# GpSimd makes the one-hots of the deep ranks for the tile that follows (graph aggregation with sampled neighbours, one core)

## What is computed

```
vals, idx = top_k(where(A != 0, -arange(N), -inf), 25)
agg = max over the valid neighbours of X[idx]
agg = where(degree <= 25, maximum(agg, 0), agg)
out = relu(concat([X, agg]) @ W + b)
return layernorm(X + out)
```

## Time and profile before

| | |
|---|---|
| median of three runs | 594.37 us |
| profiled execution | 593.69 us |
| its span, first to last instruction | 592.0 us |
| PE, VectorE (DVE), ACT, GpSimd (POOL) busy | 501.7, 529.4, 396.1, 288.7 us |
| instructions | 13844 |
| length of a batch in the middle | some 67 us |

### The profile page before, as it was taken

One profiled execution on the slowest core, in us unless ns is written; L12 is line 12 of the kernel. 1 busy time (PEld: TensorE's weight loads), 2 busy tenths in 40 slices (PEclk: granted clock), 3 DMA queues, 4 the chain that ended last, 5 costly groups with the idle time before them and its releaser, 6 DMA issues.

```text
span 592.0 us, 13844 instructions
## 1 busy us (share of the span) xinstructions
PE 501.7 (85%) x4544; PEld 340.4 (58%) x4544; DVE 529.4 (89%) x973; ACT 396.1 (67%) x751; POOL 288.7 (49%) x462
## 2 busy tenths in 40 slices
PE   1347899989988999889988999889987999889982
PEld 0115576556654677556755667556754667556761
DVE  5647999999998989999999999999998999998894
ACT  3362567657985688657886589657885589546654
POOL 2552365257633575247733566337742376336700
PEclk9998999899998999899999999899998999899997
DMA  8893244456536644366556555475445462021102
GB/s 257 212 219 105 79 133 118 99 128 160 132 75 171 135 129 101 106 156 165 113 115 173 124 113 136 96 162 171 110 117 141 135 135 65 2 60 38 50 9 73
DMA packets 91810, 71.31 MB, mean 120 GB/s; under 512 B 63651, under 2 KB 80294, under 8 KB 91686
## 3 DMA queue, kind: packets, MB, share of 16 engines
q1 hardware_dynamic: 85286, 56.77, 39.6%
q0 software_dynamic: 6400, 13.12, 8.1%
HBM read 50.99 MB, written 4.19 MB: 93 GB/s over the span
## 4 chain that ended last, share of the span: by engine, by line
PE 37%; DVE 36%; issue 12%; DVEq 7%; DMA 4%; ACT 2%; SPq 1%; POOL 0%; POOLq 0%
PE pair L1038 29%; DVE part L781 16%; DVE hot L776 5%; DVE g_feat L854 4%; DMA adj_sb<-in_adj 4%; DVEq L851 3%; DVE g_val L822 2%; DVE agg_t L881 2%; PE misc L1083 2%; DVEq L920 1%; PE p_V L1022 1%; DVE g_score L824 1%; PE misc L1084 1%; DVE hot_high L776 1%; DVEq L988 1%
## 5 line engine op out<-in xcount | busy, mean ns | idle before, releaser
L1038 PE MATMUL pair<-hot,x_part 128*128 128x128 bf16 (+3 forms) x3120 | 411.0, 280 | 37.3 <-DVE part L781 27.9
L1038 PEld LDWEIGHTS pair<-hot,x_part 128*128 128x128 bf16 x3120 | 239.1, 99 | 145.1 <-issue 51.6
L781 DVE TENSOR_REDUCE part<-pair 128x128 f32<-128x1024 f32 (+1 forms) x256 | 279.4, 1100 | 30.0 <-PE pair L1038 28.5
L479 POOL DMA_INDIRECT g_feat<-in_x,g_idx x200 | 193.6, 968 | 131.9 <-issue 86.5
L526 POOL TENSOR_TENSOR y_sb<-relu_sb,x_sb 128x128 f32<-128x128 f32 x64 | 30.0, 469 | 146.2 <-ACT relu_sb L652 145.7
L598 ACT ACTIVATE V<-p_V 128x512 bf16<-128x512 f32 x98 | 57.7, 589 | 64.9 <-PE p_V L1022 64.7
L626 ACT ACTIVATE hot<-V,first_bias 128x1024 bf16<-128x1024 bf16 x56 | 63.9, 1141 | 25.3 <-PE pair L1038 25.3
L776 DVE TENSOR_SCALAR hot<-V 128x1024 bf16<-128x1024 bf16 x224 | 80.3, 380 | 0.0
L591 ACT ACTIVATE mask<-adj_sb 128x1024 bf16<-128x1024 uint32 x56 | 58.7, 1048 | 21.9 <-DMA adj_sb<-in_adj 21.9
L641 ACT ACTIVATE hot<-distance,one 128x1024 bf16<-128x1024 bf16 x56 | 63.9, 1141 | 0.2
L634 ACT ACTIVATE distance<-V,second_bias 128x1024 bf16<-128x1024 bf16 x56 | 63.6, 1135 | 0.0
(11 more groups left out here) (88 smaller groups left out, 408.8 us busy)
## 6 DMA issues: line engine op xcount, KB each, us to landing
adj_sb<-in_adj SPq DMA_DIRECT2D x56, 512.0 KB
g_adj<-in_adj SPq DMA_DIRECT2D x8, 512.0 KB, 4.4
x_sb<-in_x SPq DMA_DIRECT2D x8, 512.0 KB, 4.6
out<-y_sb SPq DMA_DIRECT2D x7, 512.0 KB, 5.2
g_feat<-in_x,g_idx POOLq DMA_INDIRECT x200
maskT<-mask SPq DMA_TRANSPOSE x56
out<-y_sb SPq DMA_DIRECT2D x1, 448.0 KB, 3.0
w_sb<-in_W SPq DMA_DIRECT2D x1, 128.0 KB, 6.2
```

The lines of the kernel that those rows point to most:

```text
L479: pool.indirect_dma_start(out=g_feat[w][:, k, :], out_offset=None, in_=x_rows, in_offset=bass.IndirectOffsetOnAxis(ap=g_idx[w][:, k:k + 1] ...
L781: dve.tensor_reduce(part[:, par(q, s), :, p], slots_of(q, s, p).rearrange("f k i -> f i k"), AX.X, ALU.max).then_inc(s_used, 1)
L1038: last = pe.matmul(dst, x_part[:, q, part_no, kb], one_hot, start=(first and part_no == 0), stop=(final and part_no == PARTS - 1))
```

## The change

Ranks that exist in the first one or two blocks only (no block from the third on has them; `NARROW` = 2) are made by GpSimd in place of VectorE, by the same tensor_scalar. `WIDE[s]` is the number of the other ranks: 6 in tile 1, 5 in tiles 2 and 3, 4 in 4 to 7. Those from rank 2 to `WIDE` - 1 stay on VectorE: 4, 3 and 2 a tile. `NARROWS` is 6, 4 and 3. GpSimd makes them first in its step s, for tile s+1, and signals `s_narrow`, for which PE waits beside `s_hot`. The 25 gathers are split 6, 6, 6, 3, 4 over steps 1 to 5.

```diff
+NARROW = 2
-    HOTS = {s: DEPTHS[s][0] - ACT_RANKS for s in DEPTHS}
+    WIDE = {s: sum(any(d > r for d in DEPTHS[s][NARROW:]) for r in range(DEPTHS[s][0])) for s in DEPTHS}
+    HOTS = {s: WIDE[s] - ACT_RANKS for s in DEPTHS}
+    NARROWS = {s: DEPTHS[s][0] - WIDE[s] for s in DEPTHS}
...
-            GATHER = -(-K // 5)
+            GATHERS = (0, 6, 12, 18, 21, K)
...
-                gather(0, s_g0, range(GATHER * (s - 1), min(GATHER * s, K)))
+                gather(0, s_g0, range(GATHERS[s - 1], GATHERS[s]))
...
+            def narrow_hots(i, q, s):
+
+                m = pos(i, q, s)
+                wait(s_V, 2 * m + 2)
+                if m >= 2:
+                    wait(s_pair, picked_two_before(i, q, s))
+                for r in range(WIDE[s], DEPTHS[s][0]):
+                    blocks = sum(d > r for d in DEPTHS[s])
+                    dst = hot[:, par(q, s), r, 0:blocks] if r < LOW else hot_high[:, par(q, s), r - LOW, 0:blocks]
+                    pool.tensor_scalar(dst, V[:, q, s - 1, 0:blocks], float(r + 1 - MARK), None, ALU.is_equal
+                                       ).then_inc(s_narrow, 1)
...
                 for s in range(1, NT):
-                    if s <= 5:
+                    nxt = ahead(i, q, s, 1)
+                    if nxt:
+                        narrow_hots(*nxt)
+                    if s < len(GATHERS):
                         gather0(i, q, s)
...
             split_bias()
+            narrow_hots(0, 0, 1)
             run(step)
...
-            one_hots(0, 0, 1, range(ACT_RANKS, DEPTHS[1][0]))
+            one_hots(0, 0, 1, range(ACT_RANKS, WIDE[1]))
...
-                if ranks_needed(s, p) > max([ACT_RANKS] + [ranks_needed(s, g) for g in range(p)]):
-                    pe.wait_ge(s_hot, hot_no(i, q, s, ranks_needed(s, p)))
+                needed, seen = ranks_needed(s, p), max([ACT_RANKS] + [ranks_needed(s, g) for g in range(p)])
+                if needed > seen and seen < WIDE[s]:
+                    pe.wait_ge(s_hot, hot_no(i, q, s, min(needed, WIDE[s])))
+                if needed > seen and needed > WIDE[s]:
+                    pe.wait_ge(s_narrow, narrow_no(i, q, s, needed))
```

More of the change, by code:

```diff
@@ L243, in build @@
         s_hot = sem("onehots_ready")
+        s_narrow = sem("narrow_onehots_ready")
         s_pair = sem("picked")
@@ L302, in hot_no, with narrow_no @@
             return 2 * each * i + each * q + sum(HOTS[t] for t in range(1, s)) + r - ACT_RANKS
+        def narrow_no(i, q, s, r):
+            each = sum(NARROWS.values())
+            return 2 * each * i + each * q + sum(NARROWS[t] for t in range(1, s)) + r - WIDE[s]
         def ranks_needed(s, p):
```

## The result

The changed kernel takes **639.79 us** (median of six runs, 637.9 to 641.7) where the kernel before took 594.32 beside it: a ratio of 1.0775 (95% interval 1.0744 to 1.0806). The forecast was 598, with a range of 582 to 607. Slower was right, by 5 us; it is slower by 45. The profiled execution spans 637.5 us (592.0 before) at a mean granted clock of 0.936 (0.973 before).

What follows compares the result with a forecast made beforehand. VectorE was taken to bound tiles 6 and 7 through tile 1 of the next batch, PE elsewhere. A new wait of 2.0 us less 1.39 saved gives +0.6 a batch, +5 in eight: 598 us, range 582 to 607.

Steps and rivals of the forecast that it cites:

- What VectorE gives up on the path: Narrow one-hots made in VectorE's bound stretch, tiles 5, 6, 7 and 1: 1.72 us a batch, 13.8 in eight.
- It turns on one price: GpSimd's cost c of a 128-column one-hot decides: zero change at c = 0.41, full gain at c = 0.28.
- +0.6 us a batch: Change of the batch period: VectorE's new wait of 2.0 us in tile 6 less 1.39 saved behind it.
- The price of GpSimd's one-hots: Steps 2 to 5, ahead of the last gather: 0.45 us for 128 columns, 0.70 for 256, 6.85 a batch.
- The landing: After the last gather ends, its rows take up to 2.0 us to land before VectorE's maximum in tile 6.
- VectorE's savings: VectorE behind its new wait in tile 6: 0.33 + 0.63 + 0.43 = 1.39 us saved a batch.
- The blocking rival: VectorE and GpSimd block one another: 0.11 us more on each of 13 instructions, 609 us; chance 0.09.
- The signs of being wrong: Gather-to-maximum room above 2.2 us in most batches, VectorE's wide one-hots past 0.6 us, or PE waiting for GpSimd's one-hots.
- ACT gets nothing new: ACT's work is unchanged; it takes the later first split only a tile later; costed at nothing.
- Rank 3's later gap: Tiles 4 to 7: rank 3's wide one-hot comes one gap later, some 1.3 us late in tile 6, covered by PE's idle 5.6.
- Late narrow one-hots for PE: GpSimd's steps 2 to 5 pile up and PE waits in tile 5, some 1 us a batch more: 606; chance 0.04.
- Gathers in time: No new VectorE wait in tile 6: 580.6 us whole, 587.5 halfway; chance 0.22 in time or nearly.

Runs made afterwards that it cites:

- the table that takes lateness away: Changed kernel with the 25 gathers split 9, 5, 5, 3, 3 over steps 1 to 5 in place of 6, 6, 6, 3, 4: 605.2 us against 594.2 before (1.019).
- the paced run: Changed kernel with each piece of GpSimd's two splits waiting for the piece before it: 647.8 us beside a kernel before at 593.0 (1.094).

## Why the prediction was wrong

**Right.** What VectorE gives up on the path, 13.8 us in eight batches, agrees with the runs with 19 gathers (12, and 15 with rank 3 in its old gap); no run gave anything near the 43 us of the forms. The place was right too: the one-hots queue ahead of the gathers, and VectorE waits for the last one in tile 6. "It turns on one price" was right in kind.

**The step that failed** is the sum "+0.6 us a batch": the wait of 2.0 less 1.39. It should have been +6.3 in the mean. In the fifth batch, 8.1 in place of 0.6, its terms were:

- *The price of GpSimd's one-hots*, 6.85 us ahead of the last gather. From start to start they take 2.5, 2.0, 2.4 and 2.2 us in steps 2 to 5 (280.18 less 277.65, and so on), 9.2 in all: +2.3. An undisturbed one takes some 0.50 (128 columns) and 0.84 (256: 277.65 to 278.49), near my upper 0.53 and 0.80; 9 x 0.50 + 4 x 0.84 = 7.86, and the other 1.3 came where single ones took up to 1.24 beside VectorE. With these undisturbed prices my own sum gives +1.6 us a batch, 606, so that the price alone is far from the 45 us. What was absorbed came out as forecast (9.2 - 6.5 = 2.7 for my 1.24 + 1.53). I had put 0.45, between an fp32 TENSOR_SCALAR that stood alone and a run of another operation; the row of the same operation and width, 526 ns, was the one to take.
- *The landing*: 3.60 from the last gather's start to the maximum, not 0.94 + 2.0: +0.7.
- *VectorE's savings*, 1.39 a batch. The rest of the loop is 16.70 us for 16.66 before, in the mean 0.3 shorter: +1.4 here, 1.1 in the mean. Of the 1.39, 0.33 + 0.63 were to shorten this rest. VectorE does have fewer instructions there, but it now waits 1.24 us for PE's picks at 337.17 (1.19 to 1.25 in four of the six batches, none before). PE is late by then: it had started late behind the held maximum, waited 2.15 us for rank 3's one-hot and run at the lower clock; what each of these costs no run separates. Where the gathers are in time (tiles 6, 7, 1, 2 only) the rest is 15.99. The other 0.43, of tile 1, falls where the batch waits for GpSimd, and what VectorE gives there only makes a wait longer. I had seen this for the 0.33 ahead of the wait and not for what is behind it, though a batch is a loop: GpSimd's first gather hangs on `g_idx`, the next step on relu and PE of tile 1, the last gather on all between.
- *The first maximum*, held from 1.74 to 4.75, in the mean 3.40: +3.0 here. The blocking rival named this and priced it at 0.11 us for each instruction. That was the difference of two splits as GpSimd saw them; the price is VectorE's, and it comes where GpSimd is late, for then its split of eight follows without a wait and starts beside the maximum that waited for its gather.

Sum 2.3 + 0.7 + 1.4 + 3.0 = 7.4 of the 7.5 missing in this batch.

The lateness is the root: the six added gathers alone cost 24 us, and the table that takes lateness away takes back 35.

On this rival the Trainium skill (SBUF — State Buffer, the section on its two separate sides) said that the engine that starts first has the port pair for the whole instruction and the other "fully blocks". The 4.75 and 2.82 agree that VectorE is shut out, against my weight of 0.09, though for longer than one instruction: what was left of a run of eight. But 0.41 us for a one-hot beside a paced split, and 479 ns in the mean where GpSimd is on time, show that it isn't so wherever the two meet.

**The signs of being wrong.** Two of the three came. VectorE's wide one-hots went past 0.6 us (608 ns in the mean). And the room from the last gather's end to the first maximum was above 2.2 us in five of eight batches, which was to mean "faster"; but VectorE waited for the landing in all eight, so this was landing and no room. PE waited for no one-hot of GpSimd. A side sum was off by a little as well: 0.64 in place of 0.70 for the 256-column form takes 1.9 us off 598, which is 596.1 and not below 596.

**Costed at nothing, and wrong.** "ACT gets nothing new": its normalise needs VectorE's shift, which stands behind the gather wait in VectorE's queue (25.0 us, 7 times). Rank 3's later gap, "PE's 5.6 us idle [...] cover it": perhaps 3 us by the two runs with 19 gathers, whose ratios have intervals that still overlap, and PE waits 26.1 us for VectorE's wide one-hots after, none before. The clock, on which the sum has no term: behind the idle stretch shown it falls to 0.50 for some 10 us, the mean is 0.936 in place of 0.973, and PE is busy for 514.4 us in place of 501.7. These lie inside the loop's legs and are not added to them.

**Rivals.** Late narrow one-hots for PE did not come. Gathers in time did not come, but where they are made to be in time it gives what this rival said: 581.4 with 19 of them, for the forecast 580.6.

**Open.** How long a gather's landing takes when the DMA queues are fuller (2.5 to 5 us from its start to the maximum) was not tried apart. When a run on GpSimd shuts VectorE out and when it does not is open too: a wait between its pieces ends the hold in the paced run, but the split at 247.03 had none and held VectorE hardly at all; what the engines' port does in between no run shows. What the lower clock costs was not measured apart from late gathers. Why the kernel takes 691 us and more in some jobs is open as well.

## What to carry to other kernels

Before giving an idle engine more work, look for the loop that goes through it: what releases its first instruction, what hangs on its last, and how many us of wait are left between. Idle time outside that stretch (here half of GpSimd's) can't be drawn on, and once the loop is bound by that stretch, each us put into it is a us per batch and a us saved outside it none. Try then what stands in front: moving three gathers into a wait was worth 35 us, and taking over the new work only in the steps around the engine's waits, with the gathers placed anew, beat the kernel before by 10.

## What the hardware showed that was not expected

- VectorE's 128x1024 bf16 one-hot (0.42 us) takes 2.5 to 2.8 us beside a split of eight on GpSimd that starts without a wait, and 0.41 to 0.54 beside one whose pieces wait for each other; a 1.74 us maximum takes up to 4.75. In two batches of the changed kernel a split without a wait lengthens itself instead, to 4.01 us.
- Pacing GpSimd's pieces by a semaphore costs it 0.38 us apiece (6.16 against 3.09 us for eight, from start to the next instruction).
- Behind 5.99 us of idle PE the granted clock is 0.50 from 324 to 332 us, in the last 4 of them with PE busy throughout, and 1.00 again from 334.
